# A 32-row spread pair and plain transposes in the second experts of a two-layer audio tower

## The reference

```python
logits = tokens @ router_w.T
probs = softmax(logits); rw, re = top_k(probs, 2); rw = rw / rw.sum()
combine[token, re] = rw
out = tokens
for e in range(8):
    h = gelu(tokens @ w1[e] + b1[e], approximate=False)
    y = h @ w2[e] + b2[e]
    out = out + combine[:, e:e + 1] * y
```

## Time and profile before

| | us |
|---|---|
| median of 3 runs (lowest, highest) | 752.44 (750.17, 752.7) |
| the profiled execution, its own time | 751.62 |
| its span, first to last instruction | 749.8 |
| PE busy in the span | 649.9 (87%) |
| DVE busy | 570.5 (76%) |
| ACT busy | 503.1 (67%) |
| POOL busy | 334.4 (45%) |

### The profile page before, as it was taken

The page is one execution under the profiler, slowest core; times in us unless marked ns, Lnnn a source line. Parts: engine busy times, 40 slices in busy tenths (PEclk is TensorE's granted clock), DMA queues, the critical chain, the costliest instruction groups (busy, mean ns, idle before and its releaser), DMA issues.

```text
span 749.8 us, 16418 instructions
## 1 busy us (share of the span) xinstructions
PE 649.9 (87%) x4984; PEld 357.5 (48%) x4984; DVE 570.5 (76%) x1647; ACT 503.1 (67%) x1264; POOL 334.4 (45%) x417
## 2 busy tenths in 40 slices
PE   5528998999999988999999996799898888779896
PEld 5514665666666653333232225455555555453332
DVE  6675787777777776899999978589888888773653
ACT  3646877888888863567777767477777777624542
POOL 1006678788787866133333325624554545300000
PEclk9857999999999999999999998799999999965998
DMA  4030000000000002523323330000000000000001
GB/s 109 1 112 1 1 2 1 0 0 0 0 0 0 1 1 85 200 102 108 104 98 96 99 109 1 2 2 1 1 0 0 0 0 0 2 0 2 15 19 24
DMA packets 22038, 24.37 MB, mean 33 GB/s; under 512 B 12390, under 2 KB 12902, under 8 KB 21734
## 3 DMA queue, kind: packets, MB, share of 16 engines
q1 hardware_dynamic: 19751, 23.31, 9.9%
q10 hardware_dynamic: 2239, 0.49, 0.3%
HBM read 22.48 MB, written 1.31 MB: 32 GB/s over the span
## 4 chain that ended last, share of the span: by engine, by line
PE 55%; DVE 23%; issue 8%; ACT 3%; POOL 2%; DMA 2%; DVEq 0%; SPq 0%; ACTq 0%; POOLq 0%
PE ps L726 8%; PE ps L762 7%; PE ps L1563 5%; DVE big L1097 4%; PE ps L1585 4%; PE ps L720 4%; DVE big L1138 3%; DVE big L2077 3%; PE ps L1839 2%; PE ps L1569 2%; PE ps L1817 2%; PE ps L644 2%; PE ps L708 2%; PE ps L712 2%; DVE big L1055 2%
## 5 line engine op out<-in xcount | busy, mean ns | idle before, releaser
L1344 POOL TENSOR_TENSOR big<-big 128x1024 f32<-128x1024 f32 x64 | 119.8, 1893 | 45.7 <-DVE big L1158 45.7
L942 ACT ACTIVATE big<-ps,big 128x255 f32<-128x255 f32 x256 | 117.0, 483 | 12.2 <-DVE big L1152 9.7
L904 ACT ACTIVATE big<-ps,b1s 128x512 f32<-128x512 f32 x128 | 80.2, 678 | 32.5 <-PE ps L644 31.1
L1152 DVE TENSOR_REDUCE big<-ps 128x4 f32<-128x1020 f32 x64 | 75.1, 1212 | 26.7 <-PE ps L720 26.7
L1935 ACT ACTIVATE big<-ps 128x1024 f32<-128x1024 f32 x64 | 65.9, 1030 | 33.0 <-PE ps L1575 30.6
L2077 DVE TENSOR_REDUCE big<-ps 128x4 f32<-128x1020 f32 x64 | 78.0, 1219 | 6.9 <-DVE res L2134 2.5
L726 PE MATMUL ps<-cst,big 128*128 128x128 f32 x512 | 76.7, 283 | 6.3 <-POOL big L1344 2.4
L1164 DVE COPY mid<-ps 128x512 f32<-128x512 f32 x96 | 63.4, 685 | 18.3 <-PE ps L726 15.1
L726 PEld LDWEIGHTS ps<-cst,big 128*128 128x128 f32 x512 | 54.2, 140 | 40.8 <-issue 21.5
L644 PE MATMUL ps<-big,wall 64*128 64x512 f32 x256 | 72.8, 645 | 0.7 <-ACT big L875 0.7
L655 PE MATMUL ps<-big,w2s 128*64 128x512 f32 x256 | 69.9, 625 | 2.1 <-ACT big L904 1.2
(11 more groups left out here) (274 smaller groups left out, 1327.9 us busy)
## 6 DMA issues: line engine op xcount, KB each, us to landing
mid<-spread_w SPq DMA_DIRECT2D x128, 128.0 KB, 2.8
mid<-in_split_sel SPq DMA_DIRECT2D x1, 1536.0 KB, 7.4
wall<-in_w SPq DMA_DIRECT2D x1, 1280.0 KB, 6.4
out_tokens<-res SPq DMA_DIRECT2D x16, 56.0 KB, 1.6
cst<-in_consts SPq DMA_DIRECT2D x1, 520.5 KB, 5.0
pexp<-in_w_raw SPq DMA_DIRECT2D x1, 512.0 KB, 6.3
w2s<-in_w SPq DMA_DIRECT2D x1, 512.0 KB, 3.3
mid<-in_taps ACTq DMA_DIRECT2D x1, 320.0 KB, 3.9
```

The lines of the kernel that those rows point to most:

```text
L904: last = nc.scalar.activation(hid[e % 2][j], H1(e, j), ACT.Relu, bias=b1s[0][:, 2 * e + j:2 * e + j + 1])
L942: last = nc.scalar.activation(e_sb[r % 4][:, jj, tq, 0:NW], S[:, 2 * (r % 2) + jj, tq, 0:NW], ACT.Exp, scale=-1.0, bias=minus[r % 4][:, jj ...
L1152: nc.vector.tensor_reduce(minus[r % 4], S[:, 2 * a:2 * a + 2, :, 0:NW], AX.X, ALU.min).then_inc(s_mx, 1)
L1344: nc.gpsimd.tensor_tensor(e_sb[r % 4], e_sb[r % 4], bc(inverse[r % 4].unsqueeze(3), [P, 2, 2, 256]), ALU.mult).then_inc(s_A, 1)
```

## The change

The two spreads of a group run on two different row quarters of the array: pair 0 reads rows 0 to 31 of `ct` and `selb`, pair 1 rows 32 to 63, where the second copy of the weights stands. `selb` now has 64 rows, with the 0/1 pattern at row 0 and at row 32. The GpSimd copy that fills it covers 64 partitions instead of 24.

`sum_turn` does plain transposes against the identity, each of 128x128, so `YT` holds both halves of the sum for each tile, in 128 columns. `finish` adds the second half with an addition of its own, so it has three operations and not two.

```diff
-        selb = sb("selb", [3 * 8, 4, P], BF16)
+        selb = sb("selb", [2 * 32, 4, P], BF16)
...
-                    link_p(nc.gpsimd.tensor_copy(selb[0:24].rearrange("p e f -> p (e f)"), cst[0:24, o_sel1:o_sel1 + 4 * P]))
+                    link_p(nc.gpsimd.tensor_copy(selb[:].rearrange("p e f -> p (e f)"), cst[0:64, o_sel1:o_sel1 + 4 * P]))
...
                     for n in range(2):
-                        last = nc.tensor.matmul(CB(n), selb[:, 2 * g + n], ct[0:PART, c], start=True, stop=True)
+                        copy = slice(32 * n, 32 * n + 32)
+                        last = nc.tensor.matmul(CB(n), selb[copy, 2 * g + n], ct[copy, c], start=True, stop=True)
...
                     for k in range(TC):
-                        last = nc.tensor.matmul(YT[:, D * k:D * k + D], y_sb[:, P * k:P * k + P], fold[:], start=True, stop=True)
+                        last = nc.tensor.transpose(YT[:, P * k:P * k + P], y_sb[:, P * k:P * k + P], ident)
...
-                    y = YT[:, 0:TC * D].rearrange("p (t d) -> p t d", t=TC)
+                    y = YT.rearrange("p (t j d) -> p t j d", t=TC, j=2)
                     tl = slice(TC * c, TC * c + TC)
                     dve.wait_ge(s_yt, c + 1)
-                    link(nc.vector.tensor_tensor(yy, y, x2[:, tl, 0], ALU.add))
+                    link(nc.vector.tensor_tensor(yy, y[:, :, 0], x2[:, tl, 0], ALU.add))
+                    link(nc.vector.tensor_tensor(yy, yy, y[:, :, 1], ALU.add))
                     nc.vector.tensor_tensor(res[:, tl], res[:, tl], yy, ALU.add).then_inc(s_done, 1)
...
     sel1 = np.zeros((P, 4, 2, 64))
-    for part in range(3):
-        for e in range(8):
-            sel1[8 * part + e, e // 2, e % 2] = 1
+    for row in (0, 32):
+        for part in range(3):
+            for e in range(8):
+                sel1[row + 8 * part + e, e // 2, e % 2] = 1
```

More of the change, by code:

```diff
@@ L1512, in attention1_and_experts1 @@
             E = 8
-            PART = 3 * E
             half = NT // 2
```

## The result

The changed kernel took 742.88 us (median of 4 runs, 738.51 to 743.72) against 751.77 us of the kernel before (4 runs, 750.17 to 752.7): a ratio of 0.9881, 95% interval 0.9836 to 0.9926, so 1.2% faster. In a later series it took 742.51 us (12 runs, 736.59 to 748.89) beside 752.79 us (29 runs), a ratio of 0.9898 (0.9856 to 0.9941). The forecast was 747.2 us, range 744.4 to 750.4.

A forecast was written before the change was run, and what follows sets the result against it. PE was taken to bound the stage; savings of 0.60 + 0.88 + 0.20 + 1.76 + 1.76 - 0.02 = 5.2 us gave 746.4 from the profiled 751.62, or 747.2 from the median 0.82 above it; range 744.4 to 750.4.

The forecast's parts named there:

- the spreads: PE's paired spread matmuls: running together on two row quarters saves 0.22 us a pair at full clock, 0.40 at half.
- the turns: `sum_turn` on PE: four fp32 transposes in place of eight fp32 records save 0.44 us a chunk.
- the third addition: VectorE's extra addition in `finish`: 0.46 us, costing nothing in the steady part, with 0.29 us of cover left.
- GpSimd's copy: GpSimd's copy filling `selb`, at 112 us: no extra time for 64 partitions instead of 24; 1.0 us more if partitions counted.
- Steps 4 to 6 of the sum: From ScalarE's copies before 712.96 to the end: copies unchanged, eight spreads 1.76, four turns 1.76, the end -0.02 us.
- Step 3: Around `combine(1)`, where PE waits for VectorE: a saving of 0.2 us, not a half-clock spread's 0.4.
- step 1: Half clock until 693.59: three shorter spread pairs save 1.20 us, half kept if the clock rises at the same moment: 0.60.
- the clock turns out better: Rival on PE's half clock: it ends one 3.42 us stretch sooner, gaining 1.7 us; 745.5, at best 745.0; chance 0.13.
- step 2: From 693.59 to the table load of `gap(1)`: two spreads 0.44 and one turn 0.44, together 0.88 us saved.
- The slower one: Rival: transposes and shorter spreads drop PE to half clock after 712.96; 754.0 with four stretches, 757.4 with six; chance 0.05.
- The quarters did run together: Rival on PE's spread pairs: the row quarters don't run together, 3.0 us of savings are lost, 750.2; chance 0.06.
- VectorE didn't become the bound: Rival: the added `finish` addition takes twice 0.46 us, passing the 0.29 us of cover; 748.1; chance 0.04.

The follow-up runs named there:

- the fourth addition: The changed kernel with one more 128x256 VectorE addition in each `finish`, its result unread: 744.96 us against 752.79 for the kernel before, ratio 0.9914.
- turns-only runs: The kernel before with only the plain transposes and added `finish` addition, spreads serial: 751.58 and 752.66 us, ratios 1.0023 and 1.0005.
- the filler kernel: The changed kernel with five thrown-away hidden matmul pairs in PE's waits and the last stores through two queues: 741.97 us, ratio 0.9929 against the kernel before.

## Why the prediction was wrong in its size

- *What bounds the stage*, *the spreads* (0.22 a pair), *the turns* (0.44 a chunk), *the third addition* (0.46, covered): right, to 0.01 us a period in the profile. The cover of 0.29 us was 0.30, and the fourth addition showed that the two fp32 groups behind it are further cover, as written.
- *GpSimd's copy*, put at nothing: right, 603 ns against 599.
- *Steps 4 to 6 of the sum*: right, 3.5 us. Step 3, the place at `combine(1)`, gave 0.76 instead of 0.20; the half clock at 707.25 was missing there.
- **The step that failed is step 1**, "if the clock rises at the same moment", together with the rival *the clock turns out better*. I let the half-clock stretch end one piece of 3.42 us sooner at most, and that with a chance of 0.13 and 745.0 us at best. The first profile after had 13.7 us less of it (17.1 in place of 30.7), and the 3.4 at 707 were missing too. Step 1 and step 2 together were to save 1.48 us and their piece saved 7.17. The excess of 5.7 us stands in that piece: PE ran 19.3 us of it busy at half clock before and 6.0 after, and 13.3 us less at half speed is up to 6.7 us, some of it lost in waits. The unchanged kernel shows what such a stretch is worth: its profiles with 30.7 and 13.7 us of half clock differ by 7.0 in this piece. The kernel's level at equal half clock is 5.3 ± 0.5 us below that of before, which is the forecast's 5.2. The remaining 3.4 us of the 8.7 are, by the make of the fit, what 11.6 us less half-clock time come to at 0.30 us each.
- *Is it tied to the change?* The mean half-clock time of 16 runs is 11.6 ± 3.1 us lower, so it isn't only chance of four runs. In profiles, the first spread pair on two quarters goes with a short half-clock stretch, 8 of 8 against 2 of 9 (3 of 9 with the one of 23.9), and it parts the profiles without exception where half clock begins 11.1 us or more ahead of `hidden(0, 1)`, as it did in both the profile before and the first one after. Where it begins later, the stretch is short with either form, and that is chance as far as these runs show. In mean times that pair alone goes with about half of it, 5.9 ± 2.7 us, and the first three pairs with 3.1 ± 3.5, so the times neither show nor refute it. How much each other part of the change adds stays open, and why the clock rises when it does was not found.
- *The range* was built from the rivals and left out noise, beside three runs that differ by 2.5 us. The same kernel later ran between 741 and 759. A range of ±3 us was too narrow for that alone, even if the typical time had been hit.
- *The rivals.* The slower one, with the rule of the Trainium skill ("TensorE: Matmul & The Clock Gate", Part 4) that the full clock doesn't engage for transpose mode, didn't come: the steady part with its transposes ran at 1.00 in the profile after. By that rule it would have been slower. The turns-only runs had 4.3 ± 2.4 us more half-clock time than the kernel before, too near to nothing to be called an effect. The quarters did run together. VectorE didn't become the bound.

## What to carry to other kernels

In a stage where one engine has no hole, its savings can be read from start-to-start distances of the same forms elsewhere in the trace, and they arrive in full; check the cover of what is added elsewhere against the idle time that is left, and against the work behind it. Before giving a range, ask how much of the stage ran at half clock: here the same kernel took 71.3 or 62.3 us for the stage by its half-clock stretches, a difference larger than the whole change was forecast to bring. Look also at where such a stretch begins against the work: two profiles of one kernel can differ there before any changed work runs. When the play between runs is larger than the effect, compare at equal half-clock time, or piece by piece between two profiles.

## What was not expected of the hardware

- The same kernel ran between 741 and 759 us, on each of two chips, and half-clock time accounts for most of that (82% of the variance of these runs): 0.30 us for each us, 58 to 112 us of it in all but one of 122 runs.
- PE at half clock stayed there for 19 us while it was busy without a hole, and in the filler kernel it fell to half clock at 680.43, with no wait over 1.2 us since 660. The Trainium skill ("TensorE: Matmul & The Clock Gate", Part 1) names sustained activity as what releases the full clock. By these rows it didn't for 19 us.
- In 15 of 20 profiles one or two of SyncE's store issues take 0.7 to 1.7 us in place of 0.33, always the 6th or the 27th. The 27th is in the time (6.6 us behind the last addition against 5.1 to 5.3).
